# The causal mask of the attention scores as a matmul into the score bias

## The reference, cut to what matters

```
raw    = einsum('bhid,bhjd->bhij', q, k)
scores = alpha * tanh(raw / beta)
scores = scores + lam * hamming + lat          # bilinear in 12 codes per token
scores = where(causal, scores, -inf)           # j <= i only
attn   = softmax(scores, axis=-1)
out    = einsum('bhij,bhjd->bhid', attn, v)
```

## Time and profile before

| | |
|---|---|
| median of 3 runs | 1952.14 us (1948.52 to 1958.5) |
| the profiled execution | 1945.34 us |
| its span, first to last instruction | 1943.6 us |
| PE busy / PEld busy | 1751.0 us (90%) / 1045.3 us (54%) |
| DVE busy | 1307.7 us (67%) |
| ACT busy | 1233.5 us (63%) |
| POOL busy | 619.1 us (32%) |
| front stage's steps, first `tanh` to last `weighted_values` | about 94 to 1276 us |
| experts | to the end |

### The profile page before, as it was taken

One profiled execution on the slowest core, in us unless ns is written; L12 is line 12 of the kernel. 1 busy time (PEld: TensorE's weight loads), 2 busy tenths in 40 slices (PEclk: granted clock), 3 DMA queues, 4 the chain that ended last, 5 costly groups with the idle time before them and its releaser, 6 DMA issues. The chain is left out here.

```text
span 1943.6 us, 35368 instructions
## 1 busy us (share of the span) xinstructions
PE 1751.0 (90%) x11140; PEld 1045.3 (54%) x11141; DVE 1307.7 (67%) x2675; ACT 1233.5 (63%) x1260; POOL 619.1 (32%) x715
## 2 busy tenths in 40 slices
PE   4788979999599988999995999989929999999997
PEld 1333433343233333433432333358729999999997
DVE  6467758888487866878774878744456666666664
ACT  1167969999598977989895999933513333333332
POOL 0744243234325243452241212017532222222222
PEclk8778989999799998999897999999959999999998
DMA  4698685676635258786566373054147777777763
GB/s 159 192 201 175 161 156 133 150 120 151 145 59 121 85 121 186 175 164 157 134 124 123 60 180 83 17 156 145 70 159 208 197 193 208 193 194 205 195 194 88
DMA packets 183563, 288.50 MB, mean 148 GB/s; under 512 B 20832, under 2 KB 114144, under 8 KB 181280
## 3 DMA queue, kind: packets, MB, share of 16 engines
q1 hardware_dynamic: 168096, 264.92, 53.9%
q0 software_dynamic: 13440, 17.97, 5.5%
q10 hardware_dynamic: 1920, 4.23, 0.6%
HBM read 218.09 MB, written 68.96 MB: 148 GB/s over the span
## 5 line engine op out<-in xcount | busy, mean ns | idle before, releaser
L1203 DVE SCALAR_TENSOR_TENSOR probs<-probs,scal,bil_ps 128x512 f32<-128x512 f32 (+1 forms) x1152 | 789.5, 714 | 317.3 <-PE bil_ps L1045 267.4
L1124 ACT ACTIVATE probs<-probs 128x2048 f32<-128x2048 f32 (+1 forms) x288 | 522.6, 1815 | 151.9 <-DVE probs L1203 151.0
L1117 ACT ACTIVATE probs<-raw_ps 128x2048 f32<-128x2048 f32 (+1 forms) x288 | 509.4, 1769 | 36.8 <-PE raw_ps L1027 27.8
L1045 PE MATMUL bil_ps<-u_mv,w_st 50*128 50x512 f32 (+3 forms) x1280 | 468.1, 458 | 17.6 <-DVE probs L1203 13.6
L1045 PEld LDWEIGHTS bil_ps<-u_mv,w_st 50*128 50x128 f32 x1280 | 200.7, 190 | 505.0 <-DVE probs L1203 410.5
L1925 ACT ACTIVATE rows_sb<-fc_ps,b 128x128 f32<-128x128 f32 x576 | 161.0, 369 | 345.0 <-DVE hid_lo L1957 304.5
L1064 PE MATMUL o_ps<-probs,v_sb 128*32 128x512 f32 (+3 forms) x2560 | 305.3, 559 | 69.3 <-POOL probs L883 55.1
L1027 PE MATMUL raw_ps<-q_mv,k_st 64*128 64x512 f32 (+3 forms) x1280 | 273.9, 399 | 10.3 <-ACT probs L1117 7.9
L1881 PE MATMUL fc_ps<-modrow,rows_sb 128*128 128x128 f32 x2304 | 271.4, 276 | 0.0
L1881 PEld LDWEIGHTS fc_ps<-modrow,rows_sb 128*128 128x128 f32 x2304 | 265.4, 193 | 0.0
L1854 POOL DMA_INDIRECT out<-modrow,token x72 | 125.3, 1741 | 379.5 <-DVE modrow L1990 362.4
(11 more groups left out here) (233 smaller groups left out, 1540.6 us busy)
## 6 DMA issues: line engine op xcount, KB each, us to landing
rows_sb<-in_w SPq DMA_DIRECT2D x72, 1024.0 KB, 4.9
q_mv<-q_split SPq DMA_DIRECT2D x128, 128.0 KB, 7.6
k_st<-k_split SPq DMA_DIRECT2D x48, 256.0 KB, 8.6
rows<-x_rows SPq DMA_DIRECT2D x72, 130.0 KB, 2.1
v_rows<-rows_sb SPq DMA_DIRECT2D x8, 1024.0 KB, 7.4
o_t<-o_sb SPq DMA_DIRECT2D x32, 256.0 KB, 8.1
k_st<-k_split SPq DMA_DIRECT2D x16, 512.0 KB, 9.6
v_sb<-v_rows SPq DMA_DIRECT2D x8, 1024.0 KB, 13.5
```

What stands on the lines that cost most here:

```text
L1045: mm = pe.matmul(bil_ps[:, hd % 2, column:column + width], codes(kt)[row:row + BIAS_ROWS, :], u_mv[row:row + BIAS_ROWS, p, hd // 2, query: ...
L1117: act.activation(probs[:, s % NBUF, :, first:BLK], raw_ps[:, :, first:BLK], ACT.Tanh).then_inc(tanh_ready, 1)
L1124: act.activation(scores, scores, ACT.Exp).then_inc(exp_ready, 1)
L1203: dve.scalar_tensor_tensor(scores, scores, scal[:, ALPHA:ALPHA + 1], bil_ps[:, hd % 2, first:BLK], ALU.mult, ALU.add).then_inc(sum_ready, 1)
```

## The change

POOL's `mask` and its 128 `affine_select` instructions go, and with them the semaphore `mask_ready`: `weighted_values` waits for `exp_ready` in every step. In their place a constant tile `later` [128, 128] in fp32r holds 0 where the query is not before the key and -2^20 where it is. For each head and each tile of a diagonal step, right after the bias matmul, PE does one more matmul into the same `bil_ps` columns, with the identity as stationary operand (all 128 rows of the array) and `later` as moving operand (128 columns), accumulating. The exponential of such a sum is zero.

There are 4 heads x 128 tiles = 512 such matmuls. The identity must be fp32r for it: it now arrives in `ident_in` and DVE copies it to `ident_r` at the start (`ident` is the same tile seen as fp32). POOL builds `later` at the start of the front stage with a memset and an `affine_select`.

```
-    mask_ready ... MASKS_BEFORE = {s: n for n, s in enumerate(DIAG)}
+LATER = -float(1 << 20)
...
+        ident_r = sb(ctx, "ident", [P, P], F32R)
+        ident = ident_r[:, :].bitcast(F32)
...
+            dve.tensor_copy(ident_r[:, :], ident_in[:, :])
...
-            def mask(s):
-                pool.wait_ge(exp_ready, s + 1)
-                for _, column, _, _ in STEPS[s][1]:
-                    tri = probs[:, s % NBUF, :, column:column + P]
-                    ins = pool.affine_select(out=tri, in_=tri, compare_op=ALU.is_ge, fill=0.0, base=0,
-                                             pattern=[[0, HG], [1, P]], channel_multiplier=-1)
-                ins.then_inc(mask_ready, 1)
...
+            pool.memset(x_o[:, 0, 0:P], 0.0).then_inc(later_ready, 1)
+            pool.wait_ge(later_ready, 1)
+            pool.affine_select(out=later[:, :], in_=x_o[:, 0, 0:P], compare_op=ALU.is_ge, fill=LATER, base=0,
+                               pattern=[[1, P]], channel_multiplier=-1).then_inc(later_ready, 1)
...
             for s in range(NSTEP):
-                if s in MASKS_BEFORE:
-                    mask(s)
...
                         mm = pe.matmul(bil_ps[:, hd % 2, column:column + width],
                                        codes(kt)[row:row + BIAS_ROWS, :],
                                        u_mv[row:row + BIAS_ROWS, p, hd // 2, query:query + width],
-                                       start=True, stop=True)
+                                       start=True, stop=s not in DIAG)
+                        if s in DIAG:
+                            mm = pe.matmul(bil_ps[:, hd % 2, column:column + P], ident_r[:, :], later[:, :],
+                                           start=False, stop=True)
...
-                if s in MASKS_BEFORE:
-                    pe.wait_ge(mask_ready, MASKS_BEFORE[s] + 1)
-                else:
-                    pe.wait_ge(exp_ready, s + 1)
+                pe.wait_ge(exp_ready, s + 1)
```

More of the change, by code:

```diff
@@ L87 @@
 DIAG = [s for it in range(len(ITERS)) for s in range(LAST[it] - 2, LAST[it] + 1)]
-MASKS_BEFORE = {s: n for n, s in enumerate(DIAG)}
+LATER = -float(1 << 20)
 PE_LEAD = 3
@@ L203, in build @@
         modrow = sb(ctx, "modrow", [P, B * 6 * D])
-        ident = sb(ctx, "ident", [P, P])
+        ident_r = sb(ctx, "ident", [P, P], F32R)
+        ident = ident_r[:, :].bitcast(F32)
         scal = sb(ctx, "scal", [P, 16])
@@ L231, in build @@
                 front = (head_sum, soft_sum, p_in, x_in)
-                stage_modulation(nc, a, modrow, ident, scal, shift, rstd, lattice, rows_sb, front)
-                stage_front(nc, a, dram, modrow, ident, scal, shift, rstd, lattice, rows_sb, front, wo, den, ln,
+                stage_modulation(nc, a, modrow, ident_r, scal, shift, rstd, lattice, rows_sb, front)
+                stage_front(nc, a, dram, modrow, ident, ident_r, scal, shift, rstd, lattice, rows_sb, front, wo, den, ln,
                             rw1_hi, rw1_lo, x1_stored, h2_back, out)
@@ L260, in borrowed, with stage_modulation @@
     return wqkv, wcode, x_blk, xn, h, h_t, v_st
-def stage_modulation(nc, a, modrow, ident, scal, shift, rstd, lattice, rows_sb, front):
+def stage_modulation(nc, a, modrow, ident_r, scal, shift, rstd, lattice, rows_sb, front):
     with ExitStack() as ctx:
@@ L266, in stage_modulation @@
         sem = lambda n: ctx.enter_context(nc.semaphore(n))
+        ident_in = sb("ident_in", [P, P])
         wmod = sb("wmod", [P, KC, 6 * D])
@@ L296, in _ @@
             sp.dma_start(c_t[:, :, :], a["c_t"].rearrange("(k p) b -> p k b", p=P)).then_inc(c_in, 16)
-            sp.dma_start(ident[:, :], a["ident"]).then_inc(small_in, 16)
+            sp.dma_start(ident_in[:, :], a["ident"]).then_inc(small_in, 16)
             sp.dma_start(scal[:, 0:4], a["scalars"].partition_broadcast(P)).then_inc(small_in, 16)
@@ L454, in shift_of, with stage_front @@
     then_wait(pool.tensor_scalar(ln[:, :, 11], ln[:, :, 11], -1.0, 0.0, ALU.mult, ALU.add))
-def stage_front(nc, a, dram, modrow, ident, scal, shift, rstd, lattice, rows_sb, front, wo, den, ln,
+def stage_front(nc, a, dram, modrow, ident, ident_r, scal, shift, rstd, lattice, rows_sb, front, wo, den, ln,
                 rw1_hi, rw1_lo, x1_stored, h2_back, out):
@@ L492, in stage_front @@
         g_lo = sb("g_lo", [H, BLK], F32R)
+        later = sb("later", [P, P], F32R)
         x_o = sb("x_o", [P, TPB, D])
@@ L516, in stage_front @@
         raw_mm, bil_mm, pv_mm = sem("raw_mm"), sem("bil_mm"), sem("pv_mm")
-        tanh_ready, sum_ready, exp_ready, mask_ready = (
-            sem("tanh_ready"), sem("sum_ready"), sem("exp_ready2"), sem("mask_ready"))
+        tanh_ready, sum_ready, exp_ready, later_ready = (
+            sem("tanh_ready"), sem("sum_ready"), sem("exp_ready2"), sem("later_ready"))
         o_ready = sem("o_ready")
@@ L1039, in bilinear @@
                     pe.wait_ge(codes_in, 16 * N_CODES * (i + 1))
+                if s == 0:
+                    pe.wait_ge(later_ready, 2)
                 for hd in pair:
```

## The result

The changed kernel takes 2154.4 us (median of 4 runs, 2139.3 to 2162.5) against 1950.3 for the kernel before: a ratio of 1.103, 95% interval 1.096 to 1.111. It is slower by 204 us where I had forecast 115; the direction was right, the time lies 36 us above the upper end of the range. The profiled execution after took 2162.5 us with a span of 2160.7. A run more than 1.5% above the fastest of its kernel counts as slow, and the medians, ranges and ratios here and in the experiments are of the other runs.

A forecast was written before the change was run, and what follows sets the result against it. PE's program order was taken to bound the diagonal steps. Added 173 us less 15 hidden by DMA waits gave 158; 1945.3 + 158 - 39 = 2064 us against the profiled execution, stated as 2067, range 1968 to 2118.

The forecast's parts named there:

- What bounds the kernel: Attention's 288 steps: ACT sets the pace in plain steps, PE's program order is the bound in diagonal steps.
- the sign: Exponential of a second diagonal step: predicted to idle some 4 us in the later trace instead of 0.97.
- The price of a new matmul, 0.26 us: PE, diagonal steps: each identity matmul between biases holds PE 0.26 us, as the array's division changes.
- the 5.2 us per iteration: Added PE time in each of the 24 iterations with plain steps around: 6.0 us less 0.8.
- The pull-ahead: PE starts a weight load ahead of running matmuls; seen only within one division of the array.
- rival A: Identity's load hides under the bias's stream on PE: 0.11 us per matmul, 1937 us in all; chance 0.15.
- Sum 125 + 48 = 173 us: Added PE time: 5.2 us in each of 24 iterations plus 6.0 in each of 8 with diagonal steps only.
- The 15 us that DMAs would hide: First block of each batch, 8 iterations: slower PE uses 15 of some 50 idle us of DMA waits.
- The removal, 39 us: PE's 55.1 us of waits on POOL's masks go, less what the output projection then waits: 39 us gained.
- two projection waits of 5 and 14 us: Output projection would wait for POOL 5 and 14 us where the two long mask waits were.
- B: Output projection takes over the long waits, 15 us gained, 0.31 per new matmul: 2109 us, 2116 by the median; chance 0.13.
- the forecast of 119 us: Net time added over all iterations: 158 us added by the new matmuls less 39 removed with the masks.

The follow-up runs named there:

- x7: Changed kernel with each identity matmul cut to the 64 rows of the bias before it, half of the mask left out: 1930.6 us, ratio 0.989.
- x12: Changed kernel with 64-row identity matmuls in the 8 short iterations alone, half of the mask left out there: 2068.9 us.
- x1: Changed kernel without the identity matmuls, so no mask at all: 1913.5 us, ratio 0.981 to the kernel before.
- x2: Changed kernel with POOL's 128 masks and their semaphore put back, so each score is masked twice: 2153.0 us, ratio 1.102.
- x3: Changed kernel with each identity matmul replaced by two bf16 ones on the 64 rows the bias used: 1932.1 us, ratio 0.992.
- x5: Changed kernel with identity and triangle in bf16, still on all 128 rows: 2023.2 us, ratio 1.036.
- x8: Changed kernel with identity matmuls of 8 columns instead of 128, most of the mask left out: 2207.4 us, ratio 1.127.
- x4: Changed kernel with a second identity matmul after each, adding zeros to the tile's other columns: 2233.4 us, ratio 1.140.
- x13: Changed kernel with 64-row identity matmuls in the 24 long iterations alone, half of the mask left out there: 1987.7 us, ratio 1.019.

## Why the prediction was wrong

- **What bounds the kernel**, PE's order in the diagonal steps: right. ACT's waits grew with PE's stretches: by 205 us in all, 83 before exponentials and 122 before tanhs. The exponential of a second diagonal step waits 3.5 us on average (0.8 before), where the sign was some 4.
- **The price of a new matmul, 0.26 us:** right at full clock, to the last digit of the rows, and so is the 5.2 us per iteration (5.1 to 6.6 in ten of them, with the clock at or near 1.00). x7 shows that it is the division: without its change 16 matmuls cost 0.3 us and not 5.3. The pull-ahead that I had seen only within one division is there in x7, and its 1931 us are near rival A's 1937: for such a matmul A would have been the outcome.
- **The step that failed is "Sum 125 + 48 = 173 us":** it takes every duration from rows at full clock and applies it to all 32 iterations. In 8 long iterations the clock fell in or behind the diagonal steps, 53 us over the forecast, 51 of them by 0.41 us per us at low clock. The 8 short ones, with nothing but such steps, ran at a clock of 0.53 and 0.56 over two stretches of some 100 us and took 60 over it, some 59 by the same line. I had the granted clock of these places before me (the earlier trace rows have 0.75 and 0.85), and the prediction has no term for it.
- **The 15 us that DMAs would hide:** not seen by themselves. Without the some 59 us of the clock the short iterations are 34 us over before, and the forecast with the 15 taken off was 33; the estimate can't say more. In x12, with PE quick again, iterations 16 to 19 take 47.47 us and 0 to 3 take 66.50, against 51.76 and 64.54 before.
- **The removal, 39 us:** right alone (36 in x1). Beside the new matmuls the six iterations, which include the stops for values and for the multiplication, were 58 us under the pace of 5.2 where I had said 39, yet x2, with the masks back, is no slower than the change; open, see x2. Of the two projection waits of 5 and 14 us that I had named, the trace has 10.8 us in two, the longest 8.5.
- **The rivals:** B had the right sign of the error with the wrong mechanism: it gave 0.31 per matmul and a wait of the projection; neither is what the runs show. No rival had the clock in it, and the range ended at 2118 for that reason.
- **The balance** against the forecast of 119 us: +60 short, +53 long at low clock, +4 others, -19 former long waits, so 217 in the profiled execution.

What stays open: which property of the new stretches makes the clock fall. Without the added changes of division (x3, x7) it falls no more than in the kernel before: of the 12 and 10 stretches at low clock in their steps, one and none begin behind 4 us without a gap in PE's records. It falls less with loads of 0.10 us (x5), falls more with 8 columns (x8), and is not kept up by more columns (x4). This fits pauses for weight loads, but no run measured the pauses by themselves. It is also open why the clock is low in one long iteration and not in the next, which have the same instructions in the diagonal steps, and why the short iterations of x13 run at a higher clock than those after.

## What to carry to other kernels

A small matmul that is put between others is cheap if it uses the same rows of the array as its neighbours (0.02 to 0.03 us here) and dear if it doesn't (0.33 with the lost overlap, before the clock). Where a change puts loads between the streams of the bounding engine, cost it at both levels of the clock, and look at the granted clock where PE is busy, not only where it idles. And before an engine's work is moved away, look at what stands ahead of it in its queue: moving one multiplication, and the projection that waits for it, by some steps gave at least as much as taking away all the masks (41 and 36 us).

## What was unexpected of the hardware

- The granted clock went to 0.50 in stretches where PE's matmul records have no gap (4.00 of 4.00 us), and stayed there for most of 100 us in a row in the short iterations.
- Less streaming made the kernel slower: 8 columns instead of 128, 2207 us instead of 2154.
- Time against the time at 1.2 GHz lies on a line of 0.37 to 0.38 us per us for the runs of three kernels (the change, x2, x4; 0.39 to 0.45 in x5, x8, x12 and x13), with no run more than 4 us off its line. So the run-to-run spread of some 1 to 2% in them goes with the clock.
- The load of a 128 x 128 identity took 0.10 us in bf16 (x5) and 0.19 us in fp32r (the change) at full clock.
